# Layer norm before the feed-forward on ScalarE: one activation of 1024 columns, or two of 512

## What is computed

```python
x = x + 0.5 * ffn(layernorm(x)); x = x + scan(layernorm(x)); x = x + 0.5 * ffn(layernorm(x))
def ffn(x):                                   # 64 experts of rank 16, 4 of them chosen for each token
    vecs = einsum('arh,bsh->bsar', A, x)
    _, idx = top_k(norm(vecs, axis=-1), 4)
    routes = one_hot(idx, 64).sum(-2) / 4
    v = einsum('bsa,bsar->bsr', routes, vecs)
    return x @ W.T + bias + einsum('bsa,ajr,bsr->bsj', routes, B, v)
def step(h, inp):                             # the scan, over 2048 tokens; 1024 channels x 16 states
    dA_t, Bu_t, C_t = inp
    h = dA_t * h + Bu_t
    return h, sum(h * C_t[:, None, :], axis=-1)
```

## Time and profile before

| | |
|---|---|
| median of 3 runs | 2799.38 us (2798.81 to 2805.14) |
| the profiled execution | 2797.06 us, of which span 2795.3 us |
| mean granted TensorE clock | 0.985 of full speed |
| busy, share of the span | TensorE 93%, GpSimd 84%, VectorE 79%, ScalarE 54% |
| L836 | 64 instructions, 1241 ns each, 79.4 us together |

### The profile page before, as it was taken

One profiled execution on the slowest core, in us unless ns is written; L12 is line 12 of the kernel. 1 busy time (PEld: TensorE's weight loads), 2 busy tenths in 40 slices (PEclk: granted clock), 3 DMA queues, 4 the chain that ended last, 5 costly groups with the idle time before them and its releaser, 6 DMA issues.

```text
span 2795.3 us, 39869 instructions
## 1 busy us (share of the span) xinstructions
PE 2602.9 (93%) x13664; PEld 1176.9 (42%) x13664; DVE 2220.1 (79%) x2933; ACT 1496.2 (54%) x3363; POOL 2348.2 (84%) x703
## 2 busy tenths in 40 slices
PE   4989999999999999999999999999999999989999
PEld 1444444444344443444444434444444443434444
DVE  8447888888888887888878888788888888888843
ACT  5346666665555655556555555565555554655521
POOL 2138889989899898998999989999899999989910
PEclk8999999999999999999999999999999999999999
DMA  5144544544354443644544445444455434454321
GB/s 219 48 116 137 144 127 131 161 142 139 109 164 140 135 138 112 163 140 127 147 143 132 144 137 163 138 126 129 151 153 158 143 119 141 136 145 145 91 58 53
DMA packets 303520, 373.50 MB, mean 134 GB/s; under 512 B 148435, under 2 KB 220243, under 8 KB 303318
## 3 DMA queue, kind: packets, MB, share of 16 engines
q1 hardware_dynamic: 286422, 337.40, 40.5%
q10 hardware_dynamic: 16896, 33.56, 4.1%
HBM read 234.05 MB, written 103.29 MB: 121 GB/s over the span
## 4 chain that ended last, share of the span: by engine, by line
PE 22%; DVE 19%; DVEq 5%; ACT 4%; DMA 4%; issue 4%; POOL 2%; SPq 1%; ACTq 1%; POOLq 0%
DVE mreg L1147 10%; PE pv L554 7%; PE po L554 5%; PE pv L558 3%; PE po L558 3%; PE py L721 2%; ACT pA L934 2%; DMA delta_scratch<-mreg 2%; DVE pv L1108 1%; DVE sel L1105 1%; DVEq L1113 1%; DMA mreg<-xnT_scratch 1%; DVEq L1107 1%; DVEq L1063 1%; DVE sel L1116 1%
## 5 line engine op out<-in xcount | busy, mean ns | idle before, releaser
L522 POOL TENSOR_TENSOR mreg<-mreg 128x2048 f32<-128x2048 f32 x256 | 1160.9, 4535 | 37.9 <-ACT hst L920 37.8
L1147 DVE TENSOR_TENSOR_SCAN mreg<-pA,hst,mreg 128x512 f32<-128x512 f32 (+1 forms) x1024 | 1042.9, 1065 | 98.9 <-ACT pA L934 70.0
L934 ACT ACTIVATE pA<-mreg,nA 128x512 f32<-128x512 f32 (+1 forms) x1280 | 739.0, 596 | 465.9 <-DVE mreg L1147 413.2
L512 POOL TENSOR_TENSOR mreg<-mreg 128x1024 f32<-128x1024 f32 x340 | 795.3, 2363 | 226.3 <-DMA mreg<-delta_scratch 219.6
L554 PE MATMUL pv<-wA,xT 128*128 128x512 f16 x2016 | 463.2, 382 | 40.5 <-DVE xT L1085 23.8
L554 PE MATMUL po<-wB,uT 128*128 128x512 f16 x2016 | 472.1, 381 | 13.5 <-DVE xin L1071 10.2
L554 PE MATMUL po<-wW,xT 128*128 128x512 f16 x2016 | 470.1, 380 | 0.0
L506 POOL TENSOR_TENSOR mreg<-mreg 128x2048 f32<-128x2048 f32 x86 | 389.7, 4532 | 1.4 <-issue 1.4
L554 PEld LDWEIGHTS pv<-wA,xT 128*128 128x128 f16 x2016 | 191.4, 98 | 323.1 <-ACT xT L841 60.3
L554 PEld LDWEIGHTS po<-wB,uT 128*128 128x128 f16 x2016 | 192.1, 98 | 277.9 <-issue 49.4
L554 PEld LDWEIGHTS po<-wW,xT 128*128 128x128 f16 x2016 | 196.0, 98 | 238.3 <-issue 24.6
(11 more groups left out here) (132 smaller groups left out, 2404.1 us busy)
## 6 DMA issues: line engine op xcount, KB each, us to landing
mreg<-delta_scratch SPq DMA_DIRECT2D x256, 512.0 KB, 6.0
delta_scratch<-mreg ACTq DMA_DIRECT2D x128, 256.0 KB
xin<-x SPq DMA_DIRECT2D x32, 512.0 KB, 3.7
x_scratch<-xin SPq DMA_DIRECT2D x32, 512.0 KB, 6.7
xnT_scratch<-auxs SPq DMA_DIRECT2D x32, 512.0 KB, 2.9
mreg<-xnT_scratch SPq DMA_DIRECT2D x64, 256.0 KB, 6.6
yT_scratch<-mreg SPq DMA_DIRECT2D x64, 256.0 KB, 2.5
uT<-yT_scratch SPq DMA_DIRECT2D x32, 512.0 KB, 4.7
```

The source lines that it names most:

```text
L512: pool.tensor_tensor(h[:, half * n:half * n + n, :], u, b.broadcast_to([P, n, c.width]), ALU.mult).then_inc(s_bm, 1)
L522: pool.tensor_tensor(h, h, by_c, ALU.mult).then_inc(s_cm, 1)
L934: last = nc.scalar.activation(dst[:, part, :], src[:, part, :], ACT.Exp, scale=nA[:, m:m + 1])
L1147: last = V.tensor_tensor_scan(h, split(pA[:, i % 2, :], c)[:, part, :], h, before, ALU.mult, ALU.add)
```

## The change

`normed` writes xn in two instructions of 512 columns instead of one of 1024, and each adds one to s_xn, so that the semaphore counts two for a unit. TensorE waits for the first count ahead of the first four transposes and for the second ahead of the last four. VectorE's wait before it overwrites the statistics counts two for a unit as well. All else is as it was.

```diff
             def norm_blocks(b, half):
-                if half == 0:
-                    pe.wait_ge(s_xn, b.u + 1)
+                pe.wait_ge(s_xn, b.u * 2 + 1 + half)
                 if half == 0:
                     pe.wait_ge(s_u, b.u * 2)
                 blocks(ptn[half], lambda k: xn[:, (half * KB + k) * P:(half * KB + k + 1) * P], s_xT, idf[:, :])
...
             def normed(b, nT):
                 act.wait_ge(s_nT, nT)
                 act.wait_ge(s_pq, nT // 2)
-                nc.scalar.activation(xn[:, :], xin[:, b.p, :], ACT.Identity, scale=lnb["ln1"]["r"][:, :],
-                                     bias=lnb["ln1"]["nm"][:, :]).then_inc(s_xn, 1)
+                for half in range(2):
+                    cols = slice(half * HF, (half + 1) * HF)
+                    nc.scalar.activation(xn[:, cols], xin[:, b.p, cols], ACT.Identity, scale=lnb["ln1"]["r"][:, :],
+                                         bias=lnb["ln1"]["nm"][:, :]).then_inc(s_xn, 1)
...
-                dve.wait_ge(s_xn, b.u)
+                dve.wait_ge(s_xn, b.u * 2)
                 stats("ln1", xin[:, b.p, :], s_mv)
```

## The result

| | before | after |
|---|---|---|
| median, 15 runs each | 2798.93 us | 2807.35 us |
| ratio, 95% interval | | 1.0036 (1.0028 to 1.0044) |
| span of the profiled execution | 2795.3 us | 2806.4 us |

A forecast was written before the change was run, and what follows sets the result against it. The prediction took ScalarE's list, late at the decay behind L836 in a closed chain to the experts, as the bound. 37 units x 0.30 us = +11.1, with +0.8, -0.8 and -0.2, gave +10.9: median 2810 us, range 2801 to 2816.

The forecast's parts named there:

- The price on ScalarE's list: At L836: the second half ends later than the whole row did, making ScalarE's list 0.30 us later from there on.
- The fixed cost of 0.19 us: Skill page's price for an extra ScalarE instruction, 224 cycles at 1.2 GHz; by it the sum would be about +6.7 us.
- The chain and its slack: L836, decay, scan step, decay, L841, L1085, experts: no slack, experts tight behind L1085 in 46 of units 4 to 60.
- The sum's terms: Unit-by-unit gains and losses: 37 x 0.30 = +11.1, +0.8, -0.8 and -0.2 us, together +10.9 us.
- The 34 units of the sum's first line: Units with experts tight behind L1085, left of 46 after taking out 7 and 5; +0.30 us each.
- the 7 units taken out for L903: Tight units where TensorE soon waits for L903 behind a load of the tile's inputs; the 0.30 us vanishes there.
- the five taken out for GpSimd: Units 8, 16, 30, 49, 56, where TensorE or VectorE soon waits for GpSimd; left out of the 0.30 us loss.
- The units where TensorE's list was the bound: Units 18, 24, 58, 59, after a wait for L836: 4 x -0.20 = -0.8 us.
- The early transposes: Rival: TensorE's list bounds, so earlier transposes gain 0.20 us in 31 places, 2793 us, or 2786; chance 0.06.
- The swallowed delay: Rival: waits for GpSimd or DMA absorb half of the 37 units or more; +2 to +8 us, 2801 to 2807; chance 0.28.
- The cheap second half: Rival: L836's second half costs ScalarE 0.10 us net instead of 0.30; +3.4 us, 2803 us; chance 0.06.
- The signs to look for: Halves 0.81 us each; row wait down about 31 x 0.4, L1085's towards 35 us, decay waits up to 17 us larger.

The follow-up runs named there:

- The one column alone: Kernel before the change, row whole, plus a one-column ScalarE instruction with both operands in tiles right behind it; ratio 1.0033 to the kernel before.
- The kernel with one wait: Changed kernel, but TensorE waits for both halves ahead of its first transpose; ratio 1.0044 to the kernel before.
- f2: Kernel before the change with only TensorE's list changed: the eight matmuls L558 stand ahead of the eight transposes; ratio 1.0024 to the kernel before.
- the four pieces: Changed kernel with the row in four pieces of 256 columns, TensorE waiting for two, then four; ratio 1.0125 to the kernel before.

## Why the prediction was right, and where it wasn't

- **The price on ScalarE's list**, 0.30 us: measured 0.28. The halves take 807 ns each, against 814 from the line through two rows. The copy starts 0.26 to 0.29 us later, from the normalisation's start, in 51 of the units 4 to 60. The one column alone gives the same loss, so the price is what counts. The fixed cost of 0.19 us, worked out in the prediction from the Trainium skill's page "VectorE: DVE Perf Modes", section "The TRN2 errata", is too low here. The rows of one-column instructions before (busy us, mean ns) say where the difference is: 187 ns with no operand in a tile, 279 with one, 387 with two.

```profile
L815 ACT ACTIVATE ln_nm<-ln_mv 128x1 f32<-128x1 f32 x96 | 18.0, 187 | 0.0
L820 ACT ACTIVATE ln_nm<-ln_nm,ln_r 128x1 f32<-128x1 f32 x96 | 26.8, 279 | 0.0
```

- **The chain and its slack**: right. In the changed kernel 55 of the 57 units have the experts tight behind the remainder, where 46 had. The kernel with one wait shows that TensorE's early start at the transposes is worth about 3 us by the ratios, and not told from nothing; the sum had 1.0 us.
- **The sum's terms**: the total was near, +10.9 us against +8.4 us in the medians and +11.1 us in the spans, but in part by luck. From one `refine` to the next, 26 of the 57 turns grew by 0.26 to 0.29 us, together 7.2 us. The other 31 changed by -1.2 to +2.0 us, together +4.2 us. The 34 units of the sum's first line gave 10.9 us (10.2 forecast); all the other turns gave +0.5 us (+0.9 forecast), but as a sum of terms that miss by more: the 7 units taken out for L903 changed by -0.9 to +2.0 us each, +1.9 together, where I had 0, and four of the five taken out for GpSimd did come out at 0 or below, while the fifth (49) grew by its 0.29 us.
- **A second look** is the profile of the changed kernel run again: 32 of its 57 turns are within 0.02 us of the first's. The 34 units gave 9.7 us there and the others -3.2. Some large changes return (unit 37: -0.93 and -0.94 us; unit 53: +1.99 and +1.87), others don't (unit 6: +1.90 and +0.26; unit 29: -0.13 and +2.10) and so differ from execution to execution. Both are read against one profile of the kernel before, so a large change that returns can also be that profile's own. The spacing did not grow by a steady 0.2 us; that is only the mean.
- **The units where TensorE's list was the bound** (18, 24, 58, 59) were to become 0.20 us shorter. From normalisation to experts they changed by -1.17, -0.87, -0.56 and -0.23 us, in the second profile by -1.35, +1.53, -0.20 and -0.22. With the one column, where the transposes are not earlier, units 18 and 24 are shorter by 0.88 and 0.87 as well, and 58 and 59 unchanged. So 58 and 59 are of the early transposes, and the 0.20 us fits three of their four values; 18 and 24 moved by other waits, which the sum did not have.
- **The rivals.** The early transposes were excluded by the kernel with one wait and by f2. The swallowed delay, for half of the 37 units or more, was excluded by the four pieces, which lost in proportion or more. The cheap second half was excluded by the trace. The page "Perfetto Trace Analysis" of the Trainium skill, section "Optimizing Scalar/DVE Operations", says that breaking up instructions of an engine that isn't saturated but makes others idle may let work be completed sooner. The first four transposes were sooner here (0.87 us instead of 1.29), the experts later: ScalarE was 54% busy, TensorE did idle for it, and the broken-up instruction made it worse, as something more urgent was queued behind it.
- **The signs to look for**: the wait for the row was to fall by 12 us, less a new wait; it fell by 15.0. The second half's wait is 0.28 us in 32 places, where 0.2 was forecast. The wait for the remainder was to go towards 35 us; it went to 42.8. The forecast had left out that TensorE also comes earlier, and so waits longer; the kernel with one column, without the earlier transposes, has 34.8. GpSimd's wait for deltas grew, so the sign against the forecast there did not come. VectorE's waits for decays were to grow by up to 17 us; they grew by 10.4 us, and by 15.8 with those behind L920.

## What to carry to other kernels

A wait of the busiest engine is a prize only if the next wait behind it doesn't take it back: look at what ends the second one before shortening the first. When an instruction is split, count what it costs the instructions queued behind it on its own engine, and ask whether one of those is more urgent than the piece that gets ready early; here the urgent one was a decay factor, and putting it in front of the row paid together with a move on TensorE. Where two engines' lists are tight within a few tenths of a us, as here, try edits as a pair: each alone lost, and the pair gained.

## What was not expected of the hardware

A one-column instruction with both operands in tiles holds ScalarE's list up by 0.28 us (1491.11 to 1491.39), as much as the second half of a row: in a chain as tight as this one, one such column in each unit costs 0.33% of 2.8 ms. The rows of L815, L820 and L822 put 92 ns on the first operand in a tile and 108 ns on the second, as durations.
